# Linear attention: lane 1 half a period behind lane 0, all queues ordered by a table of times

## The chip, the cores and the metric

One core of a Trainium2 chip runs the whole kernel in one launch. The metric is the device time of that launch in microseconds. The shown time of the kernel before is the median of three runs.

## The reference

The reference is a decoder of two layers on x of shape 32 x 128 x 128 (32 sequences, 128 tokens, width 128), with a LayerNorm after each of six sub-blocks. The change touches the second sub-block, a pair of linear attentions and an MLP, with a context `mem` of 77 tokens a sequence:

```python
def _mhla(xq, xk, xv, Wq, Wk, Wv, Wo, masked):      # 8 heads of 16
    Q, K, V = (einsum('bsq,hqd->bhsd', x_, W) for ...)
    if masked:
        Q = Q + m            # -inf where the head column is past the token number
    A = einsum('bhsd,bhse->bhde', softmax(K / SCALE, -1), V)
    Bm = einsum('bhsd,bhde->bhse', softmax(Q / SCALE, -1), A)
    return Bm.reshape(b, w, h * dd) @ Wo.T          # the reshape mixes tokens and heads
y = _ln(y + _mhla(y, y, y, Wq1, Wk1, Wv1, Wo1, True), g1, b1)
y = _ln(y + _mhla(y, mem, mem, Wq2, Wk2, Wv2, Wo2, False), g2, b2)
h = y @ E1.T @ D1.T
y = _ln(y + (h * sigmoid(h)) @ E2.T @ D2.T, g3, b3)
# and outside: x = _layernorm(x + y)
```

## The kernel before

The kernel runs six stages one after the other, with all of x in on-chip memory; between stages all engines meet at a barrier. Each stage is a block with one written-out program per engine. There is no compiler that orders instructions across engines: an engine runs its instructions strictly in the order of its program, and semaphores (`wait_ge`, `then_inc`) make it wait for the others.

The stage in question is `linear_attention_block` (L603 to L927). The 32 sequences are 8 groups of 4. Two lanes, objects with their own buffers, semaphores and four of the eight PSUM banks, each take every second group, so a lane handles 4 groups and an iteration of the loop handles 2. Bank use within a lane is fixed, so a lane has one group at a time.

A group passes these steps. For each attention k = 1, 2:

- TensorE transposes y (`y_transposed`, L842, through the helper at L835), ScalarE copies it out (L725).
- TensorE computes the queries (L856; for k = 1 also the mask L858), then keys and values (L868). For k = 1 they come from y, for k = 2 from the transposed context.
- VectorE subtracts the maximum, for queries and keys (`less_max`, L765 and L767). ScalarE takes the exponentials (L740) and copies the values (L733).
- VectorE forms sums, reciprocals and the queries' softmax (`sums`, L775 to L781). GpSimd multiplies the keys' softmax (`keys`, L682).
- TensorE transposes the queries' softmax (`softmax_transposed`, copied by ScalarE at L746) and multiplies keys by values (`products`, L884). VectorE masks the result to its diagonal blocks (`diagonal`, L787).
- TensorE applies it (`outputs`, L893), VectorE transposes blocks for the reshape (`reshape`, L793), TensorE projects (`projection`, L904).
- VectorE adds the residual and takes statistics (`residual`, L799 with L72 and L75), GpSimd turns the variance into a reciprocal deviation (`rstd`, L82 and L84), VectorE normalises (`post_norm`, L809, which needs the mean only, and L814, which needs GpSimd's result).

Then the MLP: y transposed (copy at L727), `hidden` (L917), Silu on ScalarE (L751), `mlp_output` (L922), residual and norm as before. Last the outer sum (L820) with statistics, `rstd`, and the outer norm into X (L90). GpSimd copies the next group's rows (`rows`, L696) as soon as the outer sum is formed; SP loads the next context when the present one has been transposed (L673).

The order of each engine's program comes from one helper: a hardware loop over the iterations, in it the stages, and in each stage both lanes.

```python
with eng.Fori(0, NI) as g:
    for stage in stages:
        for L in lanes:
            stage(L, g)
```

So each engine does a step for lane 0 and at once the same step for lane 1, the lanes in lock step.

Of the kernel before, what the change touches and what calls it, by code (L numbers as in the profile page):

```python
# [57 lines left out]
def group(c, g):  # L58

    return c.X[:, bass.ds(g * GB, GB), :]  # L60
# [542 lines left out]
def linear_attention_block(c, W, wsem, wcount, out):  # L603
# [49 lines left out]
    wp, ws = c.sems("x_", "wp ws").values()  # L653
    M = c.sb("x_M", [D, 2, HID], F32, ctx)

    def run(eng, setup, stages):

        setup()
        with eng.Fori(0, NI) as g:
            for stage in stages:  # L660
                for L in lanes:
                    stage(L, g)

    with nc.Block() as block:

# [9 lines left out]
        @block.gpsimd  # L675
        def _(pool):

            def keys(k):
                def stage(L, g):
                    K = KL[k]  # L680
                    pool.wait_ge(L.s["rc"], g * 2 + k)
                    nc.gpsimd.tensor_tensor(heads(L.DD[0:K, 1]), heads(L.E[0:K, 1]), each(L.sm[0:K, 1, :], K), ALU.mult).then_inc(L.s["pk"], 1)  # L682
                return stage

            def rstd(k):
                def stage(L, g):
                    ln_rstd(pool, nc, L.ln, L.s, g * 4 + k)
                return stage

            def setup():  # L690
                for L in lanes:
                    nc.gpsimd.tensor_copy(L.Y[:, :, :], X[:, L.i * GB:(L.i + 1) * GB, :]).then_inc(L.s["ys"], 1)

            def rows(L, g):
                pool.wait_ge(L.s["y2"], g * 4 + 4)
                nc.gpsimd.tensor_copy(L.Y[:, :, :], group(c, g * LANES + (L.i + LANES))).then_inc(L.s["ys"], 1)  # L696

            stages = [keys(1), rstd(1), keys(2), rstd(2), rstd(3)]
            setup()
            with pool.Fori(0, NI - 1) as g:  # L700
                for stage in stages + [rows, rstd(4)]:
                    for L in lanes:
                        stage(L, g)
            for stage in stages + [rstd(4)]:
                for L in lanes:
                    stage(L, NI - 1)

        @block.scalar
        def _(act):
# [10 lines left out]
            def y_transposed(k):  # L720
                def stage(L, g):
                    act.wait_ge(L.s["yTp"], g * 3 + k)
                    if k < 3:

                        nc.scalar.copy(L.YT[:, :].rearrange("p (b w a) -> p b w a", b=GB, w=W8), L.bank(3).rearrange("p (b a w) -> p b w a", b=GB, w=W8)).then_inc(L.s["yT"], 1)  # L725
                    else:
                        nc.scalar.copy(L.YT[:, :], L.bank(3)).then_inc(L.s["yT"], 1)  # L727
                return stage

            def values(k):  # L730
                def stage(L, g):
                    act.wait_ge(L.s["kv"], g * 2 + k)
                    nc.scalar.copy(flat(L.V[0:KL[k], :, :]), L.bank(2, KL[k])).then_inc(L.s["vs"], 1)  # L733
                return stage

            def exps(k, i):
                def stage(L, g):
                    n = P if i == 0 else KL[k]
                    act.wait_ge(L.s["d"], g * 4 + (2 * k + i - 1))
                    nc.scalar.activation(flat(L.E[0:n, i]), flat(L.DD[0:n, i]), ACT.Exp, scale=DH ** -0.25).then_inc(L.s["e"], 1)  # L740
                return stage

            def softmax_transposed(k):
                def stage(L, g):
                    act.wait_ge(L.s["sTp"], g * 2 + k)
                    nc.scalar.copy(L.sT[:, :], L.bank(3)).then_inc(L.s["sT"], 1)  # L746
                return stage
# [2 lines left out]
                act.wait_ge(L.s["d1"], g + 1)  # L750
                nc.scalar.activation(L.hs[:, :], L.bank(1), ACT.Silu).then_inc(L.s["hs"], 1)  # L751

            attend = lambda k: [y_transposed(k), exps(k, 0), exps(k, 1), values(k), softmax_transposed(k)]
            run(act, setup, [context] + attend(1) + attend(2) + [y_transposed(3), hidden])

        @block.vector
        def _(dve):
# [26 lines left out]
            def diagonal(k):  # L784
                def stage(L, g):
                    dve.wait_ge(L.s["a"], g * 2 + k)
                    nc.vector.tensor_tensor(L.BDA[:, :, :], bd(L.bank(2)), row(W["bdm"][:, :]), ALU.mult).then_inc(L.s["bda"], 1)  # L787
                return stage
# [35 lines left out]
            def outer_norm(L, g):  # L824
                ln_apply(dve, nc, group(c, g * LANES + L.i), L.Y2, L.ln, L.s, g * 4 + 4, L.s["x"])

            attend = lambda k: [less_max(k, 0), less_max(k, 1), sums(k), diagonal(k), reshape(k), residual(k, "o", 1), post_norm(k)]
            run(dve, lambda: dve.wait_ge(wsem, wcount), attend(1) + attend(2) + [residual(3, "d2", 3), post_norm(3), outer_sum, outer_norm])

        @block.tensor  # L830
        def _(pe):
# [40 lines left out]
            def softmax_transposed(k):  # L872
                def stage(L, g):
                    pe.wait_ge(L.s["pq"], g * 2 + k)
                    transposes(L, 3, L.DD[:, 0], "sTp")
                return stage
# [45 lines left out]
                    ins = nc.tensor.matmul(L.part(3, slice(0, P), b), L.hs[:, b * P:(b + 1) * P], M[:, 1, :], start=True, stop=True)  # L922
                ins.then_inc(L.s["d2"], 1)

            attend = lambda k: [y_transposed(k), queries(k), keys_values(k), softmax_transposed(k), products(k), outputs(k), projection(k)]
            run(pe, setup, [context] + attend(1) + attend(2) + [y_transposed(3), hidden, mlp_output])
    c.end_phase(ctx)  # L927


# [1130 lines left out]
```

## Time and profile before

| | before |
|---|---|
| median of 3 runs | 2467.4 us (2460.16 to 2467.96) |
| the profiled execution | 2461.68 us |
| its span | 2459.9 us |
| mean granted TensorE clock over the span | 0.843 |
| TensorE busy over the span | 72% |
| VectorE busy over the span | 71% |
| ScalarE busy over the span | 37% |
| GpSimd busy over the span | 31% |

The span goes from the first to the last instruction. Percentages over the span average six stages with different limits, so they don't say what bounds the stage at hand, which runs from about 338 to 673.5 us; its own stretches have to be read. A granted clock of 1.0 is 2.4 GHz and 0.5 is 1.2 GHz. In the names of tiles, the lanes' numbers are left out: `x_DD` is that of lane 0 or of lane 1.

### The profile page before, as it was taken

The page shows a single profiled execution, that of the slowest core. Times are in us where ns is not written, and L with a number is a line of the kernel's source. Part 1 is how long each engine was busy: PE and PEld are TensorE (multiplying, and loading weights), DVE is VectorE, ACT ScalarE, POOL GpSimd, SP SyncE. Part 2 cuts the span into 40 slices and gives each one's busy share as a digit, 9 for nine tenths or more (in the row PEclk, how much of TensorE's full clock was granted, in tenths as well). Part 3 has the DMA queues.
Part 4 walks back from the last instruction along what each step waited for, and adds up shares of the span by engine and source line. Part 5 has one row for each costly group of instructions (what it writes and reads, how often), then busy time and mean ns, then how long its engine had stood idle before and what let it go on. Part 6 is the DMA issues. An engine that isn't in the chain of part 4 may idle for free. (4 is left out here: it accounts for less than half of the span.)

```text
span 2459.9 us, 29930 instructions
## 1 busy us (share of the span) xinstructions
PE 1764.1 (72%) x9265; PEld 1067.8 (43%) x9265; DVE 1734.7 (71%) x3480; ACT 905.9 (37%) x1382; POOL 761.7 (31%) x757
## 2 busy tenths in 40 slices
PE   7999965656499857867777877679997321788880
PEld 3555555555466512322322322256666210455550
DVE  4999967676668848788788788959996567333336
ACT  2444432121145345445435434335553221123220
POOL 3222212122200035455455455532220000344441
PEclk9999987777699968878878877979998555899995
DMA  4000000000000000000000000000001300011113
GB/s 116 1 0 0 1 11 6 0 5 0 0 1 0 2 8 1 1 1 0 0 1 0 0 0 1 0 9 6 5 3 55 126 0 0 21 34 34 33 31 106
DMA packets 38144, 37.97 MB, mean 15 GB/s; under 512 B 7400, under 2 KB 33008, under 8 KB 37536
## 3 DMA queue, kind: packets, MB, share of 16 engines
q1 hardware_dynamic: 33504, 27.50, 3.7%
q0 software_dynamic: 4544, 9.32, 1.3%
q8 instruction: 44, 0.72, 0.1%
q14 instruction: 52, 0.43, 0.1%
HBM read 25.60 MB, written 11.21 MB: 15 GB/s over the span
## 5 line engine op out<-in xcount | busy, mean ns | idle before, releaser
L1478 PE MATMUL PS<-m_hC,identf 128*128 128x512 f32 x512 | 343.1, 758 | 150.7 <-POOL m_hC L1249 114.1
L1249 POOL TENSOR_TENSOR m_hC<-m_h,m_Cs 128x512 f32<-128x512 f32 x256 | 332.8, 1307 | 309.0 <-DVE m_h L1381 264.4
L1381 DVE TENSOR_TENSOR_SCAN m_h<-m_dA,PS 128x512 f32<-128x512 f32 x256 | 312.4, 1220 | 23.2 <-issue 9.7
L1478 PEld LDWEIGHTS PS<-m_hC,identf 128*128 128x128 f32 x512 | 106.5, 230 | 302.8 <-POOL m_hC L1249 228.0
L1376 DVE TENSOR_TENSOR PS<-PS,m_DU 128x512 f32<-128x512 f32 x256 | 173.7, 678 | 70.8 <-PE PS L1451 69.4
L1321 ACT COPY m_Cs<-PS 128x512 f32<-128x512 f32 x128 | 74.7, 584 | 344.2 <-PE PS L1458 342.8
L1316 ACT ACTIVATE m_dA<-m_DT,m_A 128x508 f32<-128x508 f32 x256 | 174.9, 715 | 16.8 <-DVE m_h L1381 16.6
L1605 POOL DMA_INDIRECT e_XG<-token_rows,e_ids x71 | 69.2, 974 | 237.0 <-DVE e_ids L1746 215.6
L1759 DVE TENSOR_TENSOR e_H<-PS,e_Sg 128x512 f32<-128x512 f32 x71 | 49.1, 692 | 111.0 <-PE PS L1848 111.0
L82 POOL TENSOR_TENSOR ln_lv<-ln_mv,ln_eps 128x4 f32<-128x4 f32 x40 | 8.1, 202 | 357.8 <-DVE ln_mv L75 357.8
L1651 ACT ACTIVATE e_Sg<-PS 128x512 f32<-128x512 f32 x71 | 42.4, 597 | 197.2 <-PE PS L1847 197.2
L1610 POOL DMA_INDIRECT expert_rows<-e_Yo,e_ids x71 | 70.1, 988 | 134.2 <-DVE e_Yo L1765 130.6
L311 ACT COPY a_PT<-PS 128x1024 f32<-128x1024 f32 x63 | 63.8, 1012 | 87.0 <-PE PS L522 87.0
L278 ACT ACTIVATE a_E<-a_DD 128x1024 f32<-128x1024 f32 x64 | 67.7, 1057 | 55.1 <-DVE a_DD L380 53.9
L311 ACT COPY k_PT<-PS 77x1024 f32<-77x1024 f32 x63 | 63.5, 1008 | 61.8 <-PE PS L522 61.8
L378 DVE TENSOR_REDUCE a_mx<-PS 128x8 f32<-128x1024 f32 x64 | 77.2, 1206 | 7.7 <-PE PS L515 7.7
L384 DVE TENSOR_REDUCE a_sm<-a_E 128x8 f32<-128x1024 f32 x64 | 77.4, 1209 | 5.4 <-ACT a_E L278 5.4
L522 PE MATMUL PS<-identf,k_E 128*77 128x128 f32 x512 | 70.7, 282 | 14.0 <-ACT k_E L278 13.9
L1847 PE MATMUL PS<-e_w_wg,e_xT 128*128 x142 | 80.2, 647 | 0.0
L380 DVE TENSOR_TENSOR a_DD<-PS,a_mx 128x1024 f32<-128x1024 f32 x64 | 78.3, 1224 | 2.2
L512 PE MATMUL PS<-k_BD,k_QM 128*128 128x308 f32 x256 | 79.5, 434 | 0.0
L1148 PEld LDWEIGHTS PS<-w_ew,f_G 128*128 128x128 f32 x512 | 64.7, 191 | 32.1 <-issue 25.9
(345 smaller groups left out, 4082.5 us busy)
## 6 DMA issues: line engine op xcount, KB each, us to landing
token_rows<-X SPq DMA_DIRECT2D x2, 2048.0 KB, 12.2
e_Y<-expert_rows SPq DMA_DIRECT2D x16, 256.0 KB, 3.8
e_w_wg<-in_w_wg SPq DMA_DIRECT2D x1, 2048.0 KB, 7.9
e_w_wu<-in_w_wu SPq DMA_DIRECT2D x1, 2048.0 KB, 12.3
e_w_wd<-in_w_wd SPq DMA_DIRECT2D x1, 2048.0 KB, 16.7
out_dram<-X SPq DMA_DIRECT2D x8, 256.0 KB, 2.3
X<-in_x SPq DMA_DIRECT2D x1, 1792.0 KB, 7.2
x_Cs<-in_ctx SPq DMA_DIRECT2D x8, 154.0 KB
```

The source lines that it names most:

```text
L311: nc.scalar.copy(PT[:, u % 2], PS[0:KL, 4:6, :].rearrange("p i (h q) -> p (i h) q", q=P)).then_inc(s["pt"], 1)
L378: nc.vector.tensor_reduce(m, units(hf), AX_X, ALU.max).then_inc(s["mx"], 1)
L380: nc.vector.tensor_tensor(d, units(hf), mb, ALU.subtract).then_inc(s["d"], 1)
L384: nc.vector.tensor_reduce(sm[:, u * HU:(u + 1) * HU], E[:, u % 2], AX_X, ALU.add).then_inc(s["sm"], 1)
L512: ins = nc.tensor.matmul(scores(gp), q, BD[r, par, :, b, :], start=True, stop=cross)
L1249: nc.gpsimd.tensor_tensor(hC[:, i % ND, :], hst[:, i % ND, :], Cs[:, n % ND, :], ALU.mult).then_inc(s["hC"], 1)
L1316: nc.scalar.activation(dA[:, i % ND, :, 1:P], bl(DT[:, par, ch, :])[:, :, 1:P], ACT.Exp, scale=A[:, ch, n:n + 1]).then_inc(s["dA"], 1)
L1321: nc.scalar.copy(Cs[:, n % ND, :], bank(3)).then_inc(s["Cs"], 1)
L1376: nc.vector.tensor_tensor(bank(u), bank(1 + n % 2), DU[:, par, ch, :], ALU.mult).then_inc(s["dBu"], 1)
L1381: nc.vector.tensor_tensor_scan(hst[:, i % ND, :], dA[:, i % ND].rearrange("p b l -> p (b l)"), bank(u), 0.0, ALU.mult, ALU.add).then_inc(s ...
L1478: nc.tensor.matmul(bank(5 + ch), c.identf[:, :], hC[:, i % ND, :], start=(n == 0), stop=(n == NS - 1)).then_inc(s["yacc"], 1)
L1847: nc.tensor.matmul(bank(GATE[i % 2]), xT[:, i % 2, :], one(W["wg"][:, bass.ds(e, 1), :]), start=True, stop=True).then_inc(s["gu"], 1)
```

## The change

The hardware loop goes. The helper now unrolls all iterations in Python, gives each step a due time from a table, lane 1 later by half of a period of 36, and issues an engine's steps in order of their due times (equal times keep the order in which they were listed: earlier group first, then lane 0). `k` = 2 is 13 units after `k` = 1. The steps themselves, their buffers and semaphores are the same; the counts that they wait for become constants.

```diff
-    def run(eng, setup, stages):
+    PERIOD = 36
+    ATTEND = {"y_T": 0, "y_copy": 1, "queries": 1.5, "keys_values": 1.6, "max_q": 2.5, "max_k": 3, "exp_q": 4, "exp_k": 4.5, "values": 4.6, "sums": 5, "keys": 5.5,
+              "soft_T": 6, "products": 6.5, "soft_copy": 6.6, "diagonal": 7, "outputs": 7.5, "reshape": 8.5, "projection": 9, "residual": 10, "rstd": 11, "post": 11.5}
+    LAST = {"y_T": 26, "y_copy": 27, "hidden": 27.5, "silu": 28.3, "mlp": 29, "residual": 30, "rstd": 31, "post": 31.5, "outer_sum": 33, "rows": 33.5, "outer_rstd": 34, "outer_norm": 35}
+
+    def run(setup, attend, last, context=None):
 
         setup()
-        with eng.Fori(0, NI) as g:
-            for stage in stages:
-                for L in lanes:
-                    stage(L, g)
+        due = []
+        for g in range(NI):
+            for L in lanes:
+                base = g * PERIOD + L.i * PERIOD / LANES
+                if context:
+                    due.append((base + context[0], L, g, context[1]))
+                for k in (1, 2):
+                    due += [(base + 13 * (k - 1) + ATTEND[n], L, g, make(k)) for n, make in attend.items()]
+                due += [(base + LAST[n], L, g, stage) for n, stage in last.items()]
+        for _, L, g, stage in sorted(due, key=lambda d: d[0]):
+            stage(L, g)
...
             def rows(L, g):
-                pool.wait_ge(L.s["y2"], g * 4 + 4)
-                nc.gpsimd.tensor_copy(L.Y[:, :, :], group(c, g * LANES + (L.i + LANES))).then_inc(L.s["ys"], 1)
...
+                if g + 1 < NI:
+                    pool.wait_ge(L.s["y2"], g * 4 + 4)
+                    nc.gpsimd.tensor_copy(L.Y[:, :, :], group(c, (g + 1) * LANES + L.i)).then_inc(L.s["ys"], 1)
+
+            run(setup, {"keys": keys, "rstd": rstd}, {"rstd": rstd(3), "rows": rows, "outer_rstd": rstd(4)})
...
-            attend = lambda k: [y_transposed(k), exps(k, 0), exps(k, 1), values(k), softmax_transposed(k)]
-            run(act, setup, [context] + attend(1) + attend(2) + [y_transposed(3), hidden])
+            run(setup, {"y_copy": y_transposed, "exp_q": lambda k: exps(k, 0), "exp_k": lambda k: exps(k, 1), "values": values, "soft_copy": softmax_transposed},
+                {"y_copy": y_transposed(3), "silu": hidden}, (-0.5, context))
...
-            attend = lambda k: [less_max(k, 0), less_max(k, 1), sums(k), diagonal(k), reshape(k), residual(k, "o", 1), post_norm(k)]
-            run(dve, lambda: dve.wait_ge(wsem, wcount), attend(1) + attend(2) + [residual(3, "d2", 3), post_norm(3), outer_sum, outer_norm])
+            run(lambda: dve.wait_ge(wsem, wcount),
+                {"max_q": lambda k: less_max(k, 0), "max_k": lambda k: less_max(k, 1), "sums": sums, "diagonal": diagonal, "reshape": reshape,
+                 "residual": lambda k: residual(k, "o", 1), "post": post_norm},
+                {"residual": residual(3, "d2", 3), "post": post_norm(3), "outer_sum": outer_sum, "outer_norm": outer_norm})
...
-            attend = lambda k: [y_transposed(k), queries(k), keys_values(k), softmax_transposed(k), products(k), outputs(k), projection(k)]
-            run(pe, setup, [context] + attend(1) + attend(2) + [y_transposed(3), hidden, mlp_output])
+            run(setup, {"y_T": y_transposed, "queries": queries, "keys_values": keys_values, "soft_T": softmax_transposed, "products": products, "outputs": outputs,
+                        "projection": projection},
+                {"y_T": y_transposed(3), "hidden": hidden, "mlp": mlp_output}, (-1, context))
```

## Rows read from the trace of the kernel before

**Rows 1.** Busy us by stretch (instructions); order of engines: PE, PEld, DVE, ACT, POOL, clock.

```profile
416.74:498.64 81.90, 49.59 (x364) 44.53 (x364) 56.64 (x173) 17.30 (x28) 17.14 (x22) 0.75 0.01 4
498.64:580.50 81.86, 49.63 (x364) 44.56 (x364) 56.53 (x172) 17.31 (x28) 17.14 (x22) 0.75 0.00 0
```

**Rows 2.** Waits from 340 to 670 us: us in total, times, longest.

```profile
DVE x_BDA L787 <- PE PS L884: 31.4, 16, 2.9
DVE x_Y L799 <- PE PS L922: 19.8, 4, 5.0
...
DVE x_mx L765 <- PE PS L856: 12.8, 8, 2.9
```

**Rows 3.** Timeline, VectorE's and GpSimd's steps of an iteration: start, us, engine, line.

```profile
429.50 0.68 DVE L765 TENSOR_REDUCE x_mx<-PS 128x32 f32<-128x512 f32 x1
430.22 0.69 DVE L767 TENSOR_TENSOR x_DD<-PS,x_mx 128x512 f32<-128x512 f32 x1
...
434.41 1.27 DVE L775 TENSOR_REDUCE x_mx<-x_E 128x32 f32<-128x512 f32 x2
...
436.35 1.56 POOL L682 TENSOR_TENSOR x_DD<-x_E,x_sm 128x512 f32<-128x512 f32 x1 [9.24 <-DVE x_sm L779]
436.91 1.27 DVE L775 TENSOR_REDUCE x_mx<-x_E 128x32 f32<-128x512 f32 x2
...
448.29 0.69 DVE L799 TENSOR_TENSOR x_Y<-PS,x_Y 128x512 f32<-128x512 f32 x1 [1.23 <-PE PS L904]
...
450.25 0.66 DVE L799 TENSOR_TENSOR x_Y<-PS,x_Y 128x512 f32<-128x512 f32 x1
...
450.69 1.01 POOL L84 TENSOR_TENSOR x_ln_rs<-x_ln_lv,ln_half 128x4 f32<-128x4 f32 x1
...
452.19 1.10 DVE L809 SCALAR_TENSOR_TENSOR x_Y<-x_Y,x_ln_mv,w_g 128x128 f32<-128x128 f32 x4
...
454.39 1.13 DVE L809 SCALAR_TENSOR_TENSOR x_Y<-x_Y,x_ln_mv,w_g 128x128 f32<-128x128 f32 x4
```

**Rows 4.** Timeline, TensorE's weight loads for a step, and VectorE's steps that took results.

```profile
425.36 0.55 PEld L856 LDWEIGHTS PS<-w_wq,x_YT 128*128 128x128 f32 x2
...
428.17 0.69 DVE L765 TENSOR_REDUCE x_mx<-PS 128x32 f32<-128x512 f32 x1
...
429.20 3.65 PEld L868 LDWEIGHTS PS<-w_wkv,x_YT 128*128 128x128 f32 x32
...
440.25 3.54 PEld L884 LDWEIGHTS PS<-x_V,x_DD 128*128 128x128 f32 x16
...
442.41 0.69 DVE L787 TENSOR_TENSOR x_BDA<-PS,w_bdm 128x512 f32<-128x512 f32 x1 [2.91 <-PE PS L884]
...
446.23 3.52 PEld L904 LDWEIGHTS PS<-w_wo,x_TT 128*64 128x64 f32 x64
```

**Rows 5.** Stretches of 2 us, columns as in rows 1; the clock stands after POOL.

```profile
434.00:436.00 2.00, 0.00 (x0) 0.00 (x0) 1.97 (x4) 1.47 (x3) 0.00 (x0) 1.00 0.00 0
...
438.00:440.00 2.00, 0.45 (x2) 0.45 (x3) 1.43 (x3) 0.34 (x1) 1.15 (x1) 0.51 0.00 0
...
446.00:448.00 2.00, 2.00 (x35) 1.88 (x34) 0.88 (x2) 0.00 (x0) 0.00 (x0) 1.00 0.00 0
```

**Rows 6.** Groups from 340 to 670 us by line: busy us, mean ns | idle before.

```profile
L793 DVE STREAM_TRANSPOSE x_TT<-PS 128x512 f32<-128x512 f32 x16 | 11.5, 717 | 10.3 <-PE PS L893 10.3
...
L725 ACT COPY x_YT<-PS 128x512 f32<-128x512 f32 x16 | 9.4, 586 | 96.2 <-PE PS L835 96.2
...
L751 ACT ACT_TABLE_LOAD x4 | 5.1, 1283 | 0.1
L751 ACT ACTIVATE x_hs<-PS 128x512 f32<-128x512 f32 x8 | 4.8, 598 | 0.6
```

**Rows 7.** Timeline, VectorE's first and last instruction of the stage.

```profile
346.37 0.69 DVE L765 TENSOR_REDUCE x_mx<-PS 128x32 f32<-128x512 f32 x1 [9.19 <-PE PS L858]
...
672.36 1.11 DVE L90 TENSOR_SCALAR X<-x_Y,x_ln_mv,x_ln_rs 128x128 f32 x4 [0.41 <-POOL x_ln_rs L84]
```

More of the change, by code:

```diff
@@ L694, in rows @@
             def rows(L, g):
-                pool.wait_ge(L.s["y2"], g * 4 + 4)
-                nc.gpsimd.tensor_copy(L.Y[:, :, :], group(c, g * LANES + (L.i + LANES))).then_inc(L.s["ys"], 1)
[L698 to L706, printed above, removed]
+                if g + 1 < NI:
+                    pool.wait_ge(L.s["y2"], g * 4 + 4)
+                    nc.gpsimd.tensor_copy(L.Y[:, :, :], group(c, (g + 1) * LANES + L.i)).then_inc(L.s["ys"], 1)
+            run(setup, {"keys": keys, "rstd": rstd}, {"rstd": rstd(3), "rows": rows, "outer_rstd": rstd(4)})
         @block.scalar
```

## The prediction

> **What bounds the stage now.** The change touches only the linear-attention stage, so the first view is the busy time by stretch over its second and third loop iterations [rows 1]: one iteration, two groups, takes 81.9 us. In it VectorE is busy 56.6 us, TensorE 49.6 us at a mean granted clock of 0.75, ScalarE and GpSimd 17 us each. No engine is full. The waits [rows 2] say that VectorE is held up by TensorE's results, most of all in front of L787, and in front of L799 and L765. So this is a chain of short steps handed from engine to engine, with VectorE the engine that has most of them.
>
> To see what an order can bring, I count what VectorE needs for one group, in start-to-start times of the timeline [rows 3]: a max and a subtract take 0.72 each, so one `less_max` is 1.44 and four are 5.8; `sums` 2.5, twice, 5.0; diagonal 0.72 [rows 4] and reshape 0.75 [rows 6] with their gaps, twice, 2.9; residual with its statistics 1.96, three times, and the outer sum like it, 7.8; `post_norm` 2.2, three times, 6.6; outer norm 1.15 (1.11 busy) [rows 7]. Sum 29.3 us a group, 58.6 an iteration. VectorE therefore waits 81.9 - 58.6 = 23.3 us an iteration, 11.6 a group, and that is all the change can gain: 8 x 11.6 = 93 us at most.
>
> TensorE has two speeds. At 1.2 GHz eight products of a lane come out 2.16 us after the start (L884 to L787) and the masked queries of a lane 2.8 us after (L856 to L765). At 2.4 GHz the 32 key and value loads of both lanes take 3.65 us, 1.8 a lane, and a lane's projection comes out 2.06 us after its start (L904 to L799) [rows 3, 4]. The granted clock went to 0.5 by 438-440 after TensorE had done nothing from 434 to 436, and was back at 1.0 by 446-448, after it had worked without a pause from 440 on [rows 4, 5].
>
> **What the change does, part by part.** The work itself is the same. The stage is unrolled, lane 1 is 18 table units behind lane 0, and each engine runs its steps in order of due time. Because the offset is half of 36, the two halves of a period are the same with the lanes swapped. Call A the lane in its first attention (dues 0 to 17.5) and B the one in the rest of its second attention and its MLP. VectorE's queue in a half is, from the table: B sums, B diagonal, A max_q, A max_k, B reshape, B residual, A sums, B post, A diagonal, A reshape, A residual, A post, B residual (MLP), B post, B outer sum, A's second max_q and max_k, B outer norm. TensorE's: B transposes, B products, A queries, A keys and values, B outputs, B projection, A transposes, A products, A outputs, B's y_T, A projection, B hidden, B mlp, A's second y_T, queries, keys and values, then B's next context and y_T.
>
> I walk one half from the start of B sums, t = 0, with the durations above; "wait" is VectorE idle.
> - B sums to 2.5. The reciprocal is done at 1.9, GpSimd's multiply takes 1.56 [rows 3], products start at 3.55 and come at 5.7. B diagonal is next in VectorE's queue: **wait 3.2**, done 6.4.
> - A's queries were ready long before but stand behind the products: they start at 5.3 and come at 8.2. **Wait 1.8**, max_q done 9.6.
> - Keys and values follow. One lane is 1.8 at the high clock, about 3.5 at the low, which is twice that; the clock rises while they run, I take 2.6: here 10.85. **Wait 1.2**, max_k done 12.3.
> - B reshape to 13.05, B projection 2.06 at the high clock: **wait 2.1**, B residual done 17.1. A sums stand behind it, 17.1 to 19.6, though their exponentials were ready.
> - B post: its rstd stands on GpSimd behind A keys (due 5.5 against 6). Those run 19.05 to 20.6; the rstd's two instructions end 1.4 after their statistics [rows 3], 1.3 after the keys here, 21.9. B post's first half is done at 20.7, **wait 1.2**, done 23.1.
> - A diagonal (products 20.65 to 22.8) to 23.8. Outputs at the low clock come at 26.0: **wait 2.2**, reshape to 26.75.
> - A projection: 2.06 at the high clock, up to 3.8 at the low (no row has it low, twice its loads is the bound [rows 4]); TensorE was nearly idle from 15 to 19, so it is low again, and rises in it: 3.1. **Wait 3.1**, residual to 31.85.
> - A post directly behind its own statistics: the rstd is 0.3 late, **wait 0.3**, 34.35. B's MLP was ready at 32.5 (hidden, Silu 0.60, mlp) [rows 6]. B residual 36.3, B post with **wait 0.3** 38.8, outer sum 40.8. A's second queries, keys and values were ready, 43.65; outer norm 44.8.
> Waits 15.4, so 29.3 + 15.4 = **44.7 us for a half**, one group, against 40.95 now. The lockstep has 11.6 of waits because each TensorE step there serves two lanes and the second lane's result follows while VectorE works on the first's.
>
> **Ends of the stage.** Lane 0 runs its first attention alone: from the first max to the end of its second max_k 29.3 us (3.4 for the maxes, 2.6 sums, then products, diagonal, outputs, reshape and projection 10.4 at the low clock, residual and post 4.5, and 8.4 for y_T, queries, keys and the second maxes). Seven halves overlap. Lane 1 runs its last half alone: 2.5, 3.2 and 0.7 to diagonal, outputs 2.2, reshape 0.75, projection 3.8, residual and post 4.5, then y_T, a 0.59 copy [rows 6], hidden, Silu and mlp 6.1, then 2.0 + 2.5 + 2.0 and rstd and norm 2.5: 32.7. Now the same stretch lasts 346.4 to 673.5, 327.1 us [rows 7]. Then 29.3 + 7 x 44.7 + 32.7 = 374.9; the first max comes some 0.4 earlier, since lane 1's transposes are out of the way: 374.5, **47.4 us more**.
>
> **Small parts.** Silu and exp tables switch once per lane and group instead of once per two: four more pairs of loads of 1.28 [rows 6], 10 us of ScalarE. Each falls after a copy, while TensorE computes the input or VectorE is busy: nothing, with at most 0.8 exposed a group if that cover goes. The context loads on SP keep their order and have half a period of room: nothing. Unrolling drops four loop heads and fetches more code: between -2 and +3, taken as 0. GpSimd's row copies stay behind the outer sum: nothing.
>
> In the rows GpSimd's multiply starts at 436.35 inside VectorE's `sums` and both keep their times, 1.56 and 2.5 [rows 3]. The Trainium skill, SBUF — State Buffer, on who interferes with whom, says that a two-input VectorE operation and a GpSimd operation lock each other out of the shared port pair for the whole instruction. By that rule B sums would end about a microsecond later and the sum would be some 5 us higher. The rows speak against it, so my sum leaves it out.
>
> **The rivals.** (1) *The forecast*, in-order queues put one lane's ready step behind the other's late one: 2461.7 (profiled) + 47.4 = 2509.1. The median shown is 5.7 above that execution. (2) *Other side: the clock stays up.* Place: products, queries and outputs of every half. With half the load time, the ratio of the two levels, these come 0.95 to 1.4 earlier, and the walk gives waits 2.2, 0.6, 0.4, 2.1, 1.2, 0, 1.2, 2.1, 0.3, 0.3, so 39.9 a half; the ends shrink to 23.1 and 27.1: 329.1, 2464, no change. For: TensorE is fed in smaller pieces more often. Against: even this walk leaves it idle for 4.8 us before A's softmax transposes and 6.9 us before B's, longer than the two us and more of idle after which the clock fell [rows 5]. The Trainium skill, TensorE: Matmul & The Clock Gate, says that throttled is the default and activity releases it; that would favour the denser feed. The stage turns faster only when a half is below (327.5 - 62) / 7 = 37.9, or 50.2/7 = 39.6 with the short ends, that is with waits under 8.6 to 10.3. (3) *The clock stays down*: keys and outputs 0.9 and 1.3 later, both projections low: about 49 a half, 2540. Against: three steps of A and B stand back to back on TensorE, and such runs raised it. (4) *The overlap is better than I walk* and VectorE's waits fall to 6 a half: 35.3 x 7 + 62 = 309, 2443. Against it stand the two waits right behind `sums`, which no other step covers.
>
> **Numbers.** Forecast 0.76; an in-between of (1) and (2), 2476 to 2485, 0.04; (2) 0.10; (3) 0.05; (4) 0.05. A measurement of this kernel tells 0.3%, 7.4 us, from no change. Faster 0.05, same 0.10, slower 0.85. The range reaches from the in-between to past the forecast with both projections low (1.7 more a half, 2521): 2476 to 2528.
>
> **What would show it.** In the new trace the halves are 43 to 46 us; L787 is VectorE's largest wait, about 3 us for each second attention; L765 and L799 come next; L814 waits about a microsecond for GpSimd in half of its turns; the granted clock stays near 0.75. Wrong would be a granted clock near 1.0 in the stage, or VectorE idle under 9 us a group.

## The result, and the profile after

The changed kernel takes **2517.0 us** (median of four runs, 2513.1 to 2520.0) against 2465.7 for the kernel before in the same comparison: a ratio of 1.0211 [1.0187, 1.0234]. The forecast was 2509, the range 2476 to 2528, the chance of slower 0.85. It is slower, clear of the noise; the interval spans 2%, so whether it is slower by 2% is open. The profiled execution took 2516.5 us.

The page of the changed kernel, its span, busy times and granted clock in 40 slices:

```profile
span 2514.7 us, 29741 instructions
PE 1805.1 (72%) x9265; PEld 1100.4 (44%) x9265; DVE 1740.7 (69%) x3480; ACT 913.9 (36%) x1389; POOL 761.3 (30%) x757
PEclk9999977667669988788778778879999555799995
```

The same instructions run; TensorE is busy longer, at a lower clock. The stage lies in slices 6 to 12. Its busy time by stretch, in the kernel after, from the first max to the end of the last outer norm, and for two halves of a period (columns as in [rows 1]):

```profile
346.59:720.16 373.57, 234.07 (x1436) 204.90 (x1435) 233.32 (x680) 76.08 (x117) 67.43 (x86) 0.68 0.01 3
465.74:510.15 44.41, 29.22 (x182) 25.82 (x182) 29.15 (x85) 9.77 (x15) 8.59 (x11) 0.69 0.02 4
510.15:554.53 44.38, 29.19 (x182) 25.79 (x182) 29.15 (x85) 9.77 (x15) 8.58 (x11) 0.69 0.02 4
```

The stage lasts 373.6 us, where it was 327.1 [rows 7]: 46.5 more, with 47.4 forecast. A half is one group and takes 44.4 us; the two groups of an iteration took 81.9 [rows 1]. All seven full halves, read between the starts of the second attention's reciprocal (L783: 379.14, 421.22, 465.74, 510.15, 554.53, 598.91, 643.28, 687.65), are 42.1, 44.5 and five of 44.4, 44.1 in the mean, with 44.7 forecast. VectorE is busy 29.15 in a half and idle for the other 15.2.

The 46.5 us have two parts of about the same size. Eight groups in lock step took 327.1, 40.9 each. Now seven halves take 308.5, 3.2 more each, 22 in all. The two ends, in which one lane is alone, take the other 65.0, which is 24 more than the one lock-step group that they stand for.

The waits of VectorE in the stage, us in total, times, longest (line numbers are 5 to 7 higher than before: L787 is now L792, L799 L804, L765 L770, L793 L798, L809 L814, L814 L819; the lines of L792, of L804 from L929 and of L770 answer to [rows 2]):

```profile
DVE x_Y L804 <- PE PS L911: 39.5, 16, 3.8
DVE x_BDA L792 <- PE PS L891: 27.7, 9, 3.1
DVE x_mx L770 <- PE PS L865: 21.9, 8, 9.5
DVE x_TT L798 <- PE PS L900: 19.2, 9, 2.2
DVE x_mx L770 <- PE PS L875: 15.2, 9, 2.0
DVE x_Y L819 <- POOL x_ln_rs L84: 7.5, 24, 0.5
DVE x_Y L804 <- PE PS L929: 6.7, 1, 6.7
DVE x_mx L770 <- PE PS L863: 4.0, 1, 4.0
DVE X L90 <- POOL x_ln_rs L84: 1.4, 1, 1.4
```

The wait of 9.5 in the third line lies ahead of the first max and so ahead of the stage; 12.4 of the 21.9 count. Then the waits sum to 133.6 us, where those before sum to 93.5: 40.1 more. VectorE's own busy time has grown by 6.9, from 226.4 to 233.3, nearly all at L814 (33.8, where the same step, L809, took 26.9). Together that is 47.0, and the stage grew by 46.5.

The wait for the products (L792) has shrunk from 31.4 to 27.7, and occurs 9 times where it occurred 16 times. But the projection (L804 from L911) went from 9.8 to 39.5, the outputs (L798) from 10.3 [rows 6] to 19.2, the keys (L770 from L875) from 7.3 to 15.2. The MLP's wait (L804 from L929), 19.8 before, is left once, in the last half, where nothing is beside it.

One half of the timeline after, start, us, engine, line, shapes, and in brackets the idle time before it. B is the lane in its second attention, A the one in its first:

```profile
510.15 0.35 DVE L783 RECIPROCAL x_sm<-x_mx 128x32 f32<-128x32 f32 x1
510.79 1.56 POOL L694 TENSOR_TENSOR x_DD<-x_E,x_sm 77x512 f32<-77x512 f32 x1 [4.13 <-DVE x_sm L784]
...
514.53 0.69 DVE L792 TENSOR_TENSOR x_BDA<-PS,w_bdm 128x512 f32<-128x512 f32 x1 [3.09 <-PE PS L891]
...
516.98 0.69 DVE L770 TENSOR_REDUCE x_mx<-PS 128x32 f32<-128x512 f32 x1 [1.76 <-PE PS L865]
...
520.18 0.69 DVE L770 TENSOR_REDUCE x_mx<-PS 128x32 f32<-128x512 f32 x1 [1.79 <-PE PS L875]
...
524.33 0.69 DVE L804 TENSOR_TENSOR x_Y<-PS,x_Y 128x512 f32<-128x512 f32 x1 [2.11 <-PE PS L911]
...
528.17 0.69 DVE L786 TENSOR_TENSOR x_DD<-x_E,x_sm 128x512 f32<-128x512 f32 x1
528.21 1.56 POOL L694 TENSOR_TENSOR x_DD<-x_E,x_sm 128x512 f32<-128x512 f32 x1 [15.86 <-DVE x_sm L784]
528.78 1.94 DVE L814 SCALAR_TENSOR_TENSOR x_Y<-x_Y,x_ln_mv,w_g 128x128 f32<-128x128 f32 x4
...
531.18 1.14 DVE L819 SCALAR_TENSOR_TENSOR x_Y<-x_Y,x_ln_rs,w_b 128x128 f32<-128x128 f32 x4 [0.47 <-POOL x_ln_rs L84]
...
535.15 0.72 DVE L798 STREAM_TRANSPOSE x_TT<-PS 128x512 f32<-128x512 f32 x1 [2.23 <-PE PS L900]
...
538.35 0.69 DVE L804 TENSOR_TENSOR x_Y<-PS,x_Y 128x512 f32<-128x512 f32 x1 [2.49 <-PE PS L911]
```

These are, in order, B's products, A's queries, A's keys, B's residual, B's post (with A's keys multiply on GpSimd beside it), A's outputs and A's residual: the order of the walk.

**The other 8 us.** The span grew by 54.8 and this stage by 46.5. The rest is not here but in the fourth stage, a loop that the change does not touch. Its outer norms (L90), first and last start, before and then after:

```profile
L90 DVE TENSOR_SCALAR X<-m_Xn,ln_mv,ln_rs x32: 321/334/1296, 1007.4 to 1606.6; 128x128 f32 x24, 128x128 f32<-128x128 f32 x8
```

```profile
L90 DVE TENSOR_SCALAR X<-m_Xn,ln_mv,ln_rs x32: 322/335/1292, 1054.7 to 1660.9; 128x128 f32 x24, 128x128 f32<-128x128 f32 x8
```

599.2 has become 606.2: 7.0 us. The stretches between the stages give 0.6 and the rest of the kernel 0.7. In the fourth stage's timeline most of the additional time stands at the head of its loop as idle time with no releaser. One such place, VectorE's step before, and then ScalarE's and VectorE's after:

```profile
1099.42 0.70 DVE L1376 TENSOR_TENSOR PS<-PS,m_DU 128x512 f32<-128x512 f32 x1 [0.36 <-issue]
```

```profile
1140.71 1.33 ACT L1324 ACTIVATE m_dA<-m_DT,m_A 128x508 f32<-128x508 f32 x2 [2.11 <-issue]
...
1148.76 0.70 DVE L1384 TENSOR_TENSOR PS<-PS,m_DU 128x512 f32<-128x512 f32 x1 [2.59 <-issue]
```

It stands there twice, 184 us apart (ScalarE 2.11 and 2.14, VectorE 2.59 and 2.47), and from the scan (L1389, L1381 before) ahead of each to the next scan behind it, it is 3.1 and 3.0 us longer than before: 6 of the 7 us.

### The profile page after: what moved, and what is told of

Its sections match the earlier page's. It is cut to its first block and busy times, and to the rows that moved or that the text cites. A ratio compares the mean times of both kernels' runs of the same rounds, so it can differ in the third digit from the quotient of the medians.

```text
span 2514.7 us, 29741 instructions
## 1 busy us (share of the span) xinstructions
PE 1805.1 (72%) x9265; PEld 1100.4 (44%) x9265; DVE 1740.7 (69%) x3480; ACT 913.9 (36%) x1389; POOL 761.3 (30%) x757
## 5 line engine op out<-in xcount | busy, mean ns | idle before, releaser
L1389 DVE TENSOR_TENSOR_SCAN m_h<-m_dA,PS 128x512 f32<-128x512 f32 x256 | 312.5, 1221 | 22.1 <-issue 9.7
```

What stands on the lines that cost most here:

```text
L1389: nc.vector.tensor_tensor_scan(hst[:, i % ND, :], dA[:, i % ND].rearrange("p b l -> p (b l)"), bank(u), 0.0, ALU.mult, ALU.add).then_inc(s ...
```

## The experiments

The theory: an in-order queue puts one lane's ready step behind the other lane's late one, and half a period with this table gives 15 us of such waits a group. Rivals: the unrolling costs the time; the low clock costs it; half a period is too much in itself, whatever the table. "Stage" is from the first max's start to the last outer norm's start (326.7 before, 373.2 after), "fourth" the same for the fourth stage's norms; both come from each kernel's own trace, one execution each. Ratios are to the kernel before on the same chip, with a 95% interval. Not all runs were on the same chip, so kernels are compared by ratio.

| kernel | us | ratio | stage | fourth |
|---|---|---|---|---|
| after | 2517.0 | 1.0211 [1.0187, 1.0234] | 373.2 | 606.2 |
| e1_lag0 | 2468.0 | 1.0028 [1.0018, 1.0037] | 326.7 | 606.1 |
| e2_lag26 | 2429.5 | 0.9871 [0.9854, 0.9887] | 286.5 | 606.2 |
| e3_rstd | 2503.8 | 1.0172 [1.0155, 1.0189] | 365.9 | 605.3 |
| e4_warm | 2497.6 | 1.0141 [1.0124, 1.0158] | 357.2 | 606.1 |
| e5_loop26 | 2418.3 | 0.9830 [0.9809, 0.9850] | 288.2 | 597.8 |
| e6_qfirst | 2491.5 | 1.0120 [1.0103, 1.0137] | 349.6 | 605.3 |
| e7_opt26 | 2411.1 | 0.9791 [0.9775, 0.9807] | 277.7 | 599.3 |
| e8_opt18 | 2438.4 | 0.9903 [0.9887, 0.9920] | 299.8 | 606.0 |
| e9_lockwarm | 2455.4 | 0.9973 [0.9962, 0.9983] | 322.8 | 598.5 |
| e10_all3 | 2499.3 | 1.0152 [1.0129, 1.0175] | 361.2 | 606.2 |
| e11_two | 2493.4 | 1.0122 [1.0105, 1.0138] | 352.6 | 605.3 |
| e12_fill1 | 2481.2 | 1.0069 [1.0052, 1.0085] | 336.2 | 606.2 |

### Is it the lag or the unrolling? (e1_lag0)

```diff
-                base = g * PERIOD + L.i * PERIOD / LANES
+                base = g * PERIOD + L.i * 0
```

> The changed kernel with one number altered: lane 1 has no lag, so ties put lane 0 and lane 1 step by step beside each other, as in the loop of before, but the stage stays unrolled and sorted by the table. Theory (order of the in-order queues costs the time): back at the time of before, 2466 us, within 5. Rival (the unrolled program itself costs it, by code fetch or by tables loaded more often): it stays above 2490 us.

The stage is as long as before to the tenth of a microsecond, so with the lag gone the unrolled stage costs nothing in itself. What is left, 0.28%, is the fourth stage's 6.9 us. The waits of VectorE are those of the loop too (31.4 for the products, 19.8 for the MLP). The loss in the stage is the lag's with this table; the loss in the fourth stage is not.

### A small lag (e2_lag26) and the loop kept (e5_loop26)

The lag of 2.6 table units brings lane 1 a few steps behind lane 0, both in the same attention:

```diff
-                base = g * PERIOD + L.i * PERIOD / LANES
+                base = g * PERIOD + L.i * 2.6
```

> The changed kernel with lane 1 only 2.6 table units behind instead of 18. VectorE then takes lane 1's maxes and sums in the time in which lane 0's products and outputs are on TensorE. Theory (which step stands behind which decides, not the lag as such): VectorE's waits fall from 11.6 us a group in lock step to some 7, the stage is 300 to 320 us long against 335, total 2430 to 2450 us. Rival (any lag lets one lane's late step block the other's ready one, and adds its own end): slower than 2470 us.

The time is at the lower edge of what was expected; the stage, 286.5, is well below the expected 300 to 320. VectorE's waits in the stage of this kernel:

```profile
DVE x_BDA L792 <- PE PS L891: 36.8, 8, 5.5
...
DVE x_Y L804 <- PE PS L929: 7.8, 4, 2.9
DVE X L90 <- POOL x_ln_rs L84: 5.6, 4, 1.4
```

The products are waited for once per pair of lanes, up to 5.5 us at a time, and nearly everything else is covered. The granted clock in the stage is 0.85. The fourth stage is still 606.2, so e5 takes the same order for one iteration and leaves the loop in place (the lag is short enough that no step crosses an iteration):

```diff
+        for g in (0,):
+            for L in lanes:
+                base = g * PERIOD + L.i * 2.6
...
+        steps = [(L, stage) for _, L, _, stage in sorted(due, key=lambda d: d[0])]
+        with eng.Fori(0, NI - ("rows" in last)) as g:
+            for L, stage in steps:
+                stage(L, g)
```

> The lag of 2.6 units again, in the same order on every engine, but with the hardware loop kept: one iteration is sorted by due time and the loop repeats it. It asks where the time outside the stage comes from: in the changed kernel and in all unrolled versions the fourth stage, which no edit touches, took 605.3 to 606.2 us between its first and last outer norm against 599.2 before, with gaps of 2 us at its loop heads in which ScalarE and VectorE wait for nothing. Theory (the unrolled code shifts the loops behind it in the program, and their heads are fetched late): the fourth stage is back at 599 us, total 2420 to 2425 us. Rival (the gaps have another cause, as another phase of the clock): the fourth stage stays at 606 us, total 2429 us.

The fourth stage in e5:

```profile
L90 DVE TENSOR_SCALAR X<-m_Xn,ln_mv,ln_rs x32: 321/334/1295, 967.6 to 1565.4; 128x128 f32 x24, 128x128 f32<-128x128 f32 x8
```

It takes 597.8. All four kernels with the loop (before, e5, e7, e9) are at 597.8 to 599.3, all ten that unroll it at 605.3 to 606.2. The time of e5 is a little under what was expected. So unrolling one stage costs 7 us in another. Only this link is shown. That the loop's code comes late, as the expectation had it, is a guess that no run tests.

### One term by itself: the rstd behind the keys (e3_rstd)

```diff
-              "soft_T": 6, "products": 6.5, "soft_copy": 6.6, "diagonal": 7, "outputs": 7.5, "reshape": 8.5, "projection": 9, "residual": 10, "rstd": 11, "post": 11.5}
+              "soft_T": 6, "products": 6.5, "soft_copy": 6.6, "diagonal": 7, "outputs": 7.5, "reshape": 8.5, "projection": 9, "residual": 10, "rstd": 10.4, "post": 11.5}
```

> The changed kernel with rstd due at 10.4 instead of 11, so that on GpSimd lane B's two small rstd operations come ahead of lane A's key multiply. Theory (in-order GpSimd holds post back, 0.5 us of wait and 0.8 us of a stretched first half in each of some 7 halves): 5 to 10 us less than the changed kernel, 2507 to 2512 us. Rival (post then runs beside the multiply and both want the same port, or TensorE's result is late anyway): no gain, 2515 to 2519 us, and L819 or L814 is stretched beside L694.

The wait for the rstd at L819 is gone from B's post in these halves (7.5 us in the stage to 4.2), and the stage is 7.3 shorter. So the rstd itself is worth 3.3; the rest is TensorE's, at a granted clock of 0.72 instead of 0.68: the wait for the keys fell from 15.2 to 10.5 and for the outputs from 19.2 to 17.3, that for the projection rose from 39.5 to 41.0. One edit in the order moved the clock as well, and no run separates the two. L814 keeps its stretched form. VectorE's groups in this kernel, busy us, mean ns:

```profile
L814 DVE SCALAR_TENSOR_TENSOR x_Y<-x_Y,x_ln_mv,w_g 128x128 f32<-128x128 f32 x96 | 33.8, 410 | 0.6
```

The mean was the same 409 ns in the kernel after, and 351 in e8, where the multiply falls elsewhere. So the two parts of B's post are separate: the rstd is an order, the stretch is a collision.

### Filling TensorE's idle time (e4_warm, e9_lockwarm)

In the changed kernel 32 transposes of the identity into a free part of a bank go in front of TensorE's wait for the softmax; e9 does the same to the kernel before, for lane 0 only.

```diff
+                    for _ in range(8):
+                        for b in range(GB):
+                            nc.tensor.transpose(L.part(3, slice(0, P), b), c.identf[:, :], c.identf[:, :])
```

> The changed kernel with 32 extra transposes of the identity into bank 3 ahead of each wait for the queries' softmax, in TensorE's longest idle stretch; the output stays as it is, only TensorE's work grows. It keeps TensorE busy there, so the granted clock in the stage should rise from 0.68 to above 0.9. Theory with the clock as a part of the price: the halves go from 44.4 towards the 39.9 of the walk at the high clock, total 2475 to 2495 us. Rival (queue order alone, TensorE's speed does not matter): within 5 us of 2517. A third way: the extra transposes run at the low clock, end after the softmax is ready, and it is slower by 1 us a wait, some 15 us.

> The kernel before (lock step, loop) with 32 extra transposes of the identity ahead of lane 0's wait for the queries' softmax, in which TensorE is idle for some 4 us. Output unchanged, more work for TensorE. It asks what the clock costs the lock-step order. Theory (the granted clock is a part of the price of any order here): the stage's clock rises above 0.75, L787's waits of 2.9 and 1.0 us shrink, 10 to 20 us less than before, 2443 to 2453 us. Rival (lock step hides TensorE's speed, since the lanes' steps follow each other): within 5 us of before.

In e4 the granted clock of the stage rises from 0.68 to 0.82, where above 0.9 was expected, and the stage gets back 16 of the 46.5 us; the time misses its expectation by some 3 us. In e9 it goes from 0.75 to 0.77 and the wait for the products falls from 31.4 to 25.6, but the MLP's wait takes 3.8 back (19.8 to 23.6): the kernel gains 7 us, where 10 to 20 were expected, and only 3.9 of them in the stage; where the others come from is not shown. So TensorE kept at work takes back a third of the stage's loss in this way, and a little in lock step too. Neither kernel separates the clock from the work that was added to raise it.

### Which steps stand in the way (e6_qfirst)

A's queries were ready long before but stood behind B's products. They go in front of them, and B's diagonal behind A's queries' max:

```diff
-    ATTEND = {"y_T": 0, "y_copy": 1, "queries": 1.5, "keys_values": 1.6, "max_q": 2.5, "max_k": 3, "exp_q": 4, "exp_k": 4.5, "values": 4.6, "sums": 5, "keys": 5.5,
-              "soft_T": 6, "products": 6.5, "soft_copy": 6.6, "diagonal": 7, "outputs": 7.5, "reshape": 8.5, "projection": 9, "residual": 10, "rstd": 11, "post": 11.5}
+    ATTEND = {"y_T": 0, "y_copy": 1, "queries": 0.95, "keys_values": 1.6, "max_q": 2.5, "max_k": 3, "exp_q": 4, "exp_k": 4.5, "values": 4.6, "sums": 5, "keys": 5.5,
+              "soft_T": 6, "products": 6.5, "soft_copy": 6.6, "diagonal": 7.6, "outputs": 7.7, "reshape": 8.5, "projection": 9, "residual": 10, "rstd": 11, "post": 11.5}
```

> The changed kernel, half a period of lag, with three dues altered: queries 0.95 instead of 1.5, so that TensorE does lane A's ready queries ahead of lane B's softmax transposes and products, diagonal 7.6 and outputs 7.7 instead of 7 and 7.5, so that VectorE does A's max_q before B's diagonal. It takes away just the two waits right behind B sums, of which one is 3.1 us and the other 1.8 us a half. Theory (a ready step stands behind a late one): about 2.5 us less a half, since the queries now delay the transposes by 1.5 to 2, 2490 to 2505 us. Rival (the half-period lag costs by the ends or the clock, not by these places): 2512 to 2517 us.

As expected, the wait at L792 falls from 27.7 to 8.4 us. A half falls from 44.4 to 41.0, more than the 2.5 us expected, and the stage by 23.6. Three numbers in the table of times take back half of the stage's loss: a half is now as long as a group in lock step, and what is left, 22.9, is the ends'. The granted clock of a half went from 0.69 to 0.79 with it, so a part of the gain may be the clock's.

### Do the pieces add up? (e10_all3, e11_two, e12_fill1)

e10 has the edits of e3, e4 and e6 together; e11 those of e3 and e6; e12 is e11 with the extra transposes only ahead of each lane's first attention (`range(8 if k == 1 else 0)`).

> The changed kernel, half a period of lag, with the three edits together that were tried alone: rstd at 10.4, queries 0.95 with diagonal 7.6 and outputs 7.7, and the extra transposes ahead of the softmax transposes. Alone they brought the ratio to before from 1.021 to 1.017, 1.012 and 1.014. Theory (three separate terms of one sum): they add, ratio near 1.001, 2460 to 2472 us. Rival (the same waits counted twice, since a faster TensorE also shortens what the order exposes): at most the best of the three and a little, 2480 to 2490 us.

> Half a period of lag with both queue edits together and no extra transposes: rstd 10.4; queries 0.95, diagonal 7.6, outputs 7.7. Alone they took the ratio to before from 1.021 to 1.017 and 1.012. Theory (separate places of one sum): they add, ratio 1.006 to 1.010, 2476 to 2488 us. Rival (each lets the same later wait absorb it): no better than the queries edit alone, 2490 us.

> As the run with both queue edits, with the 32 extra transposes of the identity only ahead of the first attention's softmax transposes, where TensorE still idles for 4.8 us after the other lane's projection. In the run with all three edits the extra transposes ahead of the second attention ran behind the queries at the low clock, 5.1 us, and held up products by 4; that is avoided here. Theory (clock a separate term): products and outputs of the first attention at the high clock, 1 to 1.5 us a half less, 2468 to 2480 us. Rival (the fill gains nothing once the order is better): equal to the run with both queue edits.

They do not. e11 came out as its rival had it, no better than e6. e10 is slower than both its expectation and its rival had it: the extra transposes stand behind A's queries, so TensorE reaches them late and at the low clock (0.50 from 506 to 508 us, 0.51 from 508 to 510). Its timeline:

```profile
504.97 0.69 DVE L786 TENSOR_TENSOR x_DD<-x_E,x_sm 128x512 f32<-128x512 f32 x1
...
506.62 5.11 PEld L883 LDWEIGHTS PS<-identf 128*128 128x128 f32 x32
...
513.33 0.69 DVE L792 TENSOR_TENSOR x_BDA<-PS,w_bdm 128x512 f32<-128x512 f32 x1 [4.95 <-PE PS L894]
```

The softmax is ready at 505.7, the transposes end at 511.7, and VectorE waits 4.95 us, where it waited 0.37 in e6 (and 3.1 in the changed kernel). The clock of the stage was higher than in e6, 0.84 against 0.75, and the kernel slower: a filler must end before the real step is ready. e12, with half of the fillers, gives 12 us against e11, a little short of its expectation, at a granted clock of 0.88 from 420 to 600 us.

e11 against e6, the same stretch of 40.97 us of each, columns as in [rows 1], first e6 and then e11:

```profile
502.59:543.56 40.97, 26.17 (x183) 22.90 (x183) 29.15 (x86) 9.76 (x15) 8.57 (x11) 0.79 0.02 4
```

```profile
502.59:543.56 40.97, 26.46 (x183) 23.34 (x184) 29.23 (x86) 9.77 (x15) 8.56 (x11) 0.79 0.02 4
```

From one reciprocal (L784) to the same one a half later it is 40.97 us in e6 and 40.96 in e11, though e3's stage had gained 7 us by the earlier rstd. e11's stage is even 3.0 longer, all of it before its second half. L819's wait falls from 7.4 to 4.2 and comes back at L804 (43.4 to 45.7) and L792 (8.4 to 10.6). A wait in front of one step is worth only what the next wait behind it does not take.

### Half a period with another table (e8_opt18), and the best version (e7_opt26)

Is half a period too much, or is it this table? e8 keeps the lag of 18 and the unrolling and gives every step of the first and the second attention a time of its own (the context's are -3.72 on TensorE and -0.17 on ScalarE):

```diff
+    ATTEND = {1: {"y_T": -1.45, "y_copy": 0.0, "queries": 0.22, "keys_values": 1.39, "max_q": 2.5, "max_k": 3.28, "exp_q": 3.35, "exp_k": 3.38, "values": 6.71, "sums": 3.95, "keys": 4.7, "soft_T": 6.86, "products": 7.0, "soft_copy": 7.27, "diagonal": 7.43, "outputs": 7.78, "reshape": 8.25, "projection": 9.97, "residual": 10.01, "rstd": 10.42, "post": 10.64},
+              2: {"y_T": 12.11, "y_copy": 12.3, "queries": 13.39, "keys_values": 13.77, "max_q": 13.72, "max_k": 17.81, "exp_q": 17.33, "exp_k": 18.09, "values": 19.15, "sums": 19.04, "keys": 19.09, "soft_T": 19.45, "products": 19.71, "soft_copy": 19.7, "diagonal": 20.8, "outputs": 21.5, "reshape": 21.65, "projection": 23.64, "residual": 25.13, "rstd": 25.16, "post": 25.98}}
+    LAST = {"y_T": 26.2, "y_copy": 28.09, "hidden": 28.74, "silu": 29.11, "mlp": 29.49, "residual": 29.55, "rstd": 30.38, "post": 31.45, "outer_sum": 31.84, "rows": 34.3, "outer_rstd": 35.18, "outer_norm": 38.31}
...
+                    due += [(base + ATTEND[k][n], L, g, make(k)) for n, make in attend.items()]
```

> Unrolled, lag of half a period as in the change, but with dues moved within the allowed order so that no ready step stands behind a late one for long. Theory (the dues, not the half period, made the change slow): stage 300 to 310 us against 382 in the changed kernel, total 2430 to 2445 us, faster than before. Rival (a half-period lag is itself the loss: two half-filled ends of 29 and 33 us and few steps ready at the same time): not below 2480 us.

VectorE's waits in the stage of e8:

```profile
DVE x_Y L804 <- PE PS L911: 30.7, 11, 3.8
...
DVE x_BDA L792 <- PE PS L891: 6.1, 7, 3.1
DVE x_TT L798 <- PE PS L900: 4.5, 2, 2.2
```

Halves of 31.7 to 34.2 us, a stage of 299.8, at the lower edge of what was expected, and a kernel faster than before. So the loss of the changed kernel is in its table's times, not in half a period as such, though the ends stay (64.9 us, below).

Is it the clock that e8's table has raised? Steady halves of e4, the old table with fillers, and of e8, columns as in [rows 1]:

```profile
459.47:630.09 170.62, 131.94 (x984) 117.75 (x984) 116.57 (x342) 39.11 (x60) 34.33 (x44) 0.84 0.01 3
```

```profile
477.70:614.32 136.62, 96.73 (x711) 82.87 (x710) 115.48 (x342) 38.55 (x58) 33.67 (x43) 0.85 0.01 2
```

Each is four halves, at nearly the same granted clock, 0.84 and 0.85: 42.7 us each in e4, 34.2 in e8. The table is worth 8.5 us a half with the clock alike, so the low clock is not the whole of the loss.

e7 does the same for the lag of 2.6 with the loop kept (e5 with this table, the context's times -1.73 and 1.63):

```diff
+    ATTEND = {1: {"y_T": 0.42, "y_copy": 2.25, "queries": 2.39, "keys_values": 2.56, "max_q": 3.59, "max_k": 3.74, "exp_q": 4.21, "exp_k": 4.9, "values": 5.68, "sums": 5.31, "keys": 5.55, "soft_T": 5.85, "products": 6.52, "soft_copy": 6.24, "diagonal": 6.75, "outputs": 8.28, "reshape": 8.71, "projection": 9.55, "residual": 9.72, "rstd": 10.4, "post": 11.81},
+              2: {"y_T": 14.23, "y_copy": 14.39, "queries": 15.49, "keys_values": 15.64, "max_q": 16.13, "max_k": 16.89, "exp_q": 16.78, "exp_k": 16.93, "values": 19.04, "sums": 18.68, "keys": 19.14, "soft_T": 19.74, "products": 21.08, "soft_copy": 21.32, "diagonal": 21.23, "outputs": 22.18, "reshape": 22.6, "projection": 23.85, "residual": 24.0, "rstd": 25.33, "post": 25.59}}
+    LAST = {"y_T": 27.31, "y_copy": 27.85, "hidden": 28.62, "silu": 28.95, "mlp": 29.12, "residual": 29.57, "rstd": 30.1, "post": 30.86, "outer_sum": 32.12, "rows": 33.81, "outer_rstd": 36.27, "outer_norm": 36.84}
```

> The loop with a lag of 2.6 units and dues moved by hand and search within the allowed order, separately for the two attentions: queries, keys and values of both lanes closer together, lane 1's sums before lane 0's diagonal, outputs later. Theory (VectorE's waits can be filled further; it needs 29.3 us a group, 235 us in all): stage 275 to 285 us, total 2400 to 2412 us. Rival (the rest of the waits is the chain of one group, which no order shortens): as e5, 2420 to 2425 us.

The waits of VectorE in its stage (L797 is the products, L809 the projection):

```profile
DVE x_BDA L797 <- PE PS L896: 14.2, 8, 2.5
DVE x_Y L809 <- PE PS L916: 12.1, 8, 2.8
```

The stage takes 277.7 us and the kernel 2411.1, a ratio of 0.9791 [0.9775, 0.9807]: the best of all, and better than both kernels, and within what was expected. The small lag beats the long one in the stage by its ends, and outside it by the loop kept (6.7 us in the fourth stage). From the first to the last reciprocal of a second attention e8 takes seven halves, 379.1 to 614.0 us, 67.1 for two; e7 takes 277.7 / 4 = 69.4 for an iteration, ends and all. But the ends of e8, in which one lane is alone, are 299.8 - 234.9 = 64.9 us more, nearly what they are in the changed kernel (65.0). Better tables may exist.

## Why the prediction was right

- **The mechanism and its place.** Right. The waits of a half, forecast and then measured: products 3.2 and 3.09, A's queries 1.8 and 1.76, A's keys 1.2 and 1.79, B's residual 2.1 and 2.11, A's outputs 2.2 and 2.23, A's residual 3.1 and 2.49. With the 0.84 of L814 (below) and two waits of 0.25 they make 15.3, where 15.4 were forecast. e1 shows that the lag makes the stage's loss, e6 that one pair of places in the queues carries half of it. The queues are not all of the forecast, though: its own sum has 62 us for the two ends against 41 for a group, so 21 of its 47.4 come from a lane being alone, and 24 were measured.
- **The keys and A's projection.** Off by 0.6 each, in opposite directions. In both I took a time between the two clock levels because no row had the step while the clock rises.
- **B's post.** The size was right (1.2 forecast, 0.84 + 0.47 measured), the reason half wrong. 0.47 is the wait for the rstd; the 0.84 is L814, whose four instructions take 1.94 instead of 1.10 while GpSimd multiplies. The step that failed is "The rows speak against it, so my sum leaves it out": those rows show sum reductions beside the multiply, and the two-input step that the trace has there as well (L781, at 436.30) starts before the multiply, not after it. In e8, where another step stands behind the multiply, L814 keeps its time. That the size came out is luck.
- **The ends.** 29.3 + 32.7 forecast; 31.2 (346.6 to the second attention's sums at 377.8) and 33.8 (686.3 to 720.2) measured, 3.0 too little. With halves 0.6 too long, seven times, the errors nearly cancel: 46.5 against 47.4. That it is so close is luck.
- **The unrolling.** "between -2 and +3, taken as 0" failed: 7 us, and not in the stage but in a later loop. I had looked for its price only where the code changed. This is most of the 8 us by which 2517 exceeds 2509.
- **The clock.** "stays near 0.75" failed: 0.68 in the stage. The halves came out right all the same; the walk had priced products, queries and outputs at the low level already, and their waits are those forecast. Rival (2) asked for a clock near 1.0 and fell. (Its waits as listed sum to 10.4, which makes 39.7 a half and not 39.9; nothing hangs on it.)
- **Rival (4)** was given 0.05 because "the two waits right behind `sums`, which no other step covers" stood against it. As the change stands that is so. But e8 covers them by moving other steps, and its steady halves of 34.2 are below the 35.3 that the rival asked for: the waits belonged to the table, not to the chain.
- **Signs.** Halves 44 (43 to 46 forecast); products 3.1 for each second attention, but the projection, waited for in both lanes, is the largest in total (39.5) where I named L787; the MLP's wait went as walked. The wait for GpSimd behind L814, about a microsecond in the forecast, is 0.47 and 0.25.

## What to carry to other kernels

When two lanes share in-order engines, walk one period engine by engine: each step begins at the later of its input and the step in front of it, and a ready step behind a late one is the cost; half a period apart is not in itself better or worse than lock step. Count the ends apart from the halves: with eight groups they cost 24 us here under either table, which only shorter halves can pay for. Test single places in the order (three due times gave 24 us of stage here) before giving up the lag, try a small lag that keeps the ends short and the loop rolled, and count a saved wait only after the next one. Filler work on TensorE pays only where it ends before the next real step is ready.

## What was not expected of the hardware

**A collision of VectorE and GpSimd.** The four instructions of L814 in one half of the kernel after, from 528 to 531 us (duration ns min/median/max):

```profile
L814 DVE SCALAR_TENSOR_TENSOR x_Y<-x_Y,x_ln_mv,w_g x4: 338/339/1149, 528.8 to 530.4; 128x128 f32<-128x128 f32 x4
```

Three take 0.34 us. One takes 1.15, and the group began 0.57 after GpSimd's multiply, which ends at 528.21 + 1.56 = 529.77. It is so in each of the seven full halves, of this kernel and of e3 and e6: 0.8 us each time, 5.7 of the 6.9 us by which VectorE's busy time in the stage grew. The Trainium skill, SBUF — State Buffer, on who interferes with whom, says that an exclusive lock on a shared port pair goes to whichever of the two operations starts first, and the other blocks. For L814 the trace agrees; for L786, two inputs in SBUF as well and begun 0.04 us before the multiply, the rows show that L786 keeps its 0.69. Whether the multiply is held up by it they cannot show: in every kernel here the multiply begins 0.04 to 0.05 us behind this step and lasts 1.56, and none stands alone.

In e8 the multiply falls beside another step, the outer norm, and the stretch goes there. L814 has no instruction above 0.39 us in e8, and L90, begun 0.56 us after the multiply, takes 1.85 or 1.86 us for its four, seven times, where it took 1.11 before [rows 7]:

```profile
512.24 1.56 POOL L694 TENSOR_TENSOR x_DD<-x_E,x_sm 77x512 f32<-77x512 f32 x1 [1.98 <-DVE x_sm L784]
```

```profile
512.80 1.85 DVE L90 TENSOR_SCALAR X<-x_Y,x_ln_mv,x_ln_rs 128x128 f32<-128x128 f32 x4
```

So the stretch belongs to the meeting, not to L814.

**A loop that pays for another's code.** The fourth stage, with not a line changed, takes 598 to 599 us or 605 to 606, by whether an earlier stage is a loop or unrolled, with idle time of 2.1 us (ScalarE) and 2.6 (VectorE) at its loop's head. What fills it is open.

**Periods that do not move.** e6 and e11 have different orders on GpSimd and the same half, to 10 ns (40.97 and 40.96). So has the kernel before, with yet another order: 81.92 and 81.91 for two groups in its last two periods, 40.96 each. e4's halves alternate, 44.05 and 41.25, and the pair repeats to 20 ns. I take it that the period settles where TensorE's clock rises and falls at the same place in each half; the granted clock is 0.79 in both. No run tests that, and it stays open. If it is so, what a small change of order gains or loses can vanish in the period or come out larger, and e3, e6 and e11 are to be read with that in mind.
